# Constant products behind each item's sums on TensorE in the first ten laps

## The chip, the cores and the metric

The kernel runs on one core of a Trainium2 chip. The metric is the device time of one execution in microseconds (us). A core has five engines that run side by side and wait for each other through semaphores: TensorE (PE in the rows; PEld is its loading of weights), VectorE (DVE), ScalarE (ACT), GpSimd (POOL) and SyncE (SP). TensorE's clock is granted at one of two levels, 2.4 GHz (1.00 in the profile) and 1.2 GHz (0.50).

## What is computed

A graph layer and a mixture of experts on 12500 nodes of 256 numbers and 200000 edges that are sorted by `dst`:

```python
ft = (layernorm(x) @ W).reshape(n, 4, 64)
e = leaky_relu(sum(ft * w_att_src)[src] + sum(ft * w_att_dst)[dst])
a = exp(e - emax[dst]) / segment_sum(ex, dst)[dst] * dist
x = x + segment_sum(ft[src] * a, dst)
...
x = x + sum over the top 2 of 6 experts of gate * expert(layernorm(x))
```

Everything is float32. The part that the change touches is the segment sum.

## The kernel before

A first part of the program makes a table with one row of 264 numbers for each node and plans the work. The main stage (`main_stage`) then goes over the edges, and the last part (`experts`) over the routed tokens.

In the main stage the edges come in 196 groups of 1024 edges, which are 8 tiles of 128. A block is 128 destination nodes. An item is one group together with one block that it touches; there are 294 items, 98 times three (`HI`), and the loops hold seven such threes in their body (`TURNS`), so that each engine runs 14 laps of 21 items. An item is full when it uses all 8 tiles of its group, and half when it uses 4.

For each group GpSimd issues 8 indirect DMAs (L422) that gather the rows of `src` into one of four slots (`RING`). SyncE frees a slot when the items that use it have been weighted (L977 and L978). For item k:

- ScalarE makes `by_node`, a one-hot of the nodes for each edge (L1230, L1233), three items ahead.
- TensorE's `look_up` (L1357 to L1365) takes the scores of the destination nodes with 24 small bf16 products into the PSUM bank `m_E`. In the loop it is run for item k+2, just ahead of the sums of item k.
- VectorE adds scores (L1040), takes the exponentials from ScalarE, multiplies the gathered rows by the weights into `msg` (L1064), and makes the one-hot `by_edge` (L1026).
- TensorE's `sum_up` (L1367 to L1378) sums the messages to the nodes: 8 or 4 float32 products of 128x128 by 128x260 into columns 0 to 259 of the PSUM bank `m_A`. It is written out three times, for a full item and for either half, each behind an `If`. The last product raises the semaphore `summed`.
- VectorE adds these columns to the running sums (`add_sums`, L1080 to L1085), in its item k+2.

There are three banks `m_A`. Their upper columns are used too: 320 to 351 hold the weights `wd`, 360 to 367 the local node numbers `in_block`, both written and read by VectorE alone (L928, L929).

Between `look_up` and `sum_up` TensorE loads two words of the plan into registers and, when a pair of blocks is complete, runs one step of its router: `turn` (L1380), `router` (L1389) or `score` (L1396). So in the loop the order on TensorE is: look up item k+2, words of the plan and perhaps a router step, sum item k, look up item k+3, and so on. Each of the others is its own queue in the same order of items.

Of the kernel before, what the change touches and what calls it, by code (L numbers as in the profile page):

```python
# [8 lines left out]
ALU = mybir.AluOpType  # L9
# [12 lines left out]
NB = -(-N // P)  # L22
# [4 lines left out]
MSG = D + HEADS  # L27
# [10 lines left out]
HI = CI // 2  # L38
# [5 lines left out]
READY = NODE_AT + 2 * NW  # L44
NIT = NSLOT // HI
TURNS = 7
DUE = READY + NIT + 2
REL = DUE + NIT + 1
PLAN = REL + NG
# [15 lines left out]
RSQRT_BITS = float(0x5f3759df)  # L65
assert NIT % TURNS == 0 and NG % RING == 0 and NQ * HB == NB and NQ % 2 == 0 and NCH * CI >= NI and EW == 2 * GE and NB % 2 == 0

# [823 lines left out]
def main_stage(nc, K, table, x, sched, ydram, w, out):  # L891


    with ExitStack() as ctx:
# [16 lines left out]
        r1, r2, rb = K.r1, K.r2, K.rb  # L911
# [7 lines left out]
        plan = sb("plan", [1, PLAN], I32)  # L919
# [4 lines left out]
        psA = [bank(f"A{i}") for i in range(3)]  # L924
# [72 lines left out]
        def _(dve):  # L997
# [170 lines left out]
            dve.reg_mov(done, 0)  # L1168
            with nc.Fori(0, NIT // TURNS, engines=(mybir.EngineType.DVE,), hint_back_edge=True) as lap:
                for turn_of_lap in range(TURNS):  # L1170
                    it = lap * TURNS + turn_of_lap
                    for i in range(HI):
# [29 lines left out]
        def _(act):  # L1202
# [90 lines left out]
            act.reg_mov(routed, 0)  # L1293
            with nc.Fori(0, NIT // TURNS, engines=(mybir.EngineType.Activation,), hint_back_edge=True) as lap:
                for turn_of_lap in range(TURNS):
                    it = lap * TURNS + turn_of_lap
# [22 lines left out]
                    now = count(done)  # L1319
                    act.load([due_pairs], plan[0:1, bass.ds(it + DUE, 1)])  # L1320
                    act.reg_alu(due_now, due_pairs, 0, ALU.max)
# [25 lines left out]
        @block.tensor  # L1347
        def _(pe):
            t = nc.tensor
            words = [[pe.alloc_register(f"pe_word{q}{i}") for i in range(2)] for q in range(3)]  # L1350
            done, routed, ready_pairs, due_pairs, due_now = [
                pe.alloc_register("pe_" + n) for n in ("done", "routed", "ready", "due", "due_now")]

            def fetch(q, k):
                pe.load(words[q], plan[0:1, bass.ds(k * 2 + LOOK_AT, 2)])

            def look_up(k, i, b):  # L1357

                pe.wait_ge(node_onehots, k + 1)
                for j in range(GT):  # L1360
                    for n in range(3):
                        m = t.matmul(psE[i][:, 8 * j:8 * j + 8], by_node[i][:, j * P:(j + 1) * P],  # L1362
                                     look_parts[:, bass.ds(b, 1), 8 * n:8 * n + 8].rearrange("p a n -> p (a n)"),
                                     start=(n == 0), stop=(n == 2))
                m.then_inc(looked_up, 1)  # L1365

            def sum_up(k, i, half):  # L1367


                for case, tiles in ((0, range(GT)), (1, range(GT // 2, GT)), (2, range(GT // 2))):  # L1370
                    with pe.If(half == case):
                        pe.wait_ge(edge_onehots, k + 1)
                        pe.wait_ge(weighted, k + 1)
                        pe.wait_ge(added, k + 1)
                        for j in tiles:
                            m = t.matmul(psA[i][:, 0:MSG], by_edge[i][:, j, :], msg[i][:, j, :],  # L1376
                                         start=(j == tiles[0]), stop=(j == tiles[-1]))
                        m.then_inc(summed, 1)  # L1378

            def turn(pair):  # L1380

                pe.wait_ge(y_made, pair + 1)
                for c in range(2):
                    for i in range(2):
                        m = t.transpose(psT[:, c * 2 * P + i * P:c * 2 * P + (i + 1) * P], y[:, i, c * P:(c + 1) * P],
                                        K.ident[:, :])
                m.then_inc(y_turned, 1)

            def router(pair):  # L1389
                pe.wait_ge(y_copied, pair + 1)  # L1390
                pe.wait_ge(lg_copied, pair + 1)
                for c in range(2):
                    m = t.matmul(psR[:, 0:2 * P], r1[:, c, :], yT[:, c, :], start=(c == 0), stop=(c == 1))
                m.then_inc(rh_made, 1)

            def score(pair):  # L1396
                pe.wait_ge(rh_copied, pair + 1)
                pe.wait_ge(lg_copied, pair + 1)
                for i in range(2):
                    m = t.matmul(ps_logits[:, i, 0:NX], rhT[:, i * P:(i + 1) * P], r2[:, :], start=True, stop=True)  # L1400
                m.then_inc(logits, 1)

            def route(pair):
                turn(pair)
                router(pair)
                score(pair)

            count = lambda r: pe.snap(r, min_val=0, max_val=NPAIR)
            index = lambda r: pe.snap(r, min_val=0, max_val=NPAIR - 1)

            pe.wait_ge(ready, 1)

            t.nop().then_inc(summed, 1)
            for i in (1, 2):
                t.matmul(psA[i][:, 0:MSG], sums[:, 0, 0:P], sums[:, 0, :], start=True, stop=True).then_inc(summed, 1)
            t.nop().then_inc(y_turned, 1)
            t.nop().then_inc(lg_copied, 1)
            pe.wait_ge(plan_in, 16)
            pe.wait_ge(look_steps, 7)
            pe.wait_ge(weights_in, 16 * ROUTER_LOADS)  # L1420
            first = [pe.alloc_register(f"pe_first{i}") for i in range(2)]
            for i in range(2):
                pe.load([first[i]], plan[0:1, NODE_AT + 2 * i + 1:NODE_AT + 2 * i + 2])
                look_up(i, i, pe.snap(first[i], min_val=0, max_val=NB))
            fetch(0, 0)
            pe.reg_mov(done, 0)
            pe.reg_mov(routed, 0)
            with nc.Fori(0, NIT // TURNS, engines=(mybir.EngineType.PE,), hint_back_edge=True) as lap:
                for turn_of_lap in range(TURNS):
                    it = lap * TURNS + turn_of_lap  # L1430
                    for i in range(HI):
                        k = it * HI + i
                        half = pe.snap(words[i][0], min_val=0, max_val=2)
                        look_up(k + 2, (i + 2) % 3, pe.snap(words[i][1], min_val=0, max_val=NB))
                        fetch((i + 1) % 3, k + 1)
                        if i == 0:
                            pe.load([ready_pairs], plan[0:1, bass.ds(it + READY, 1)])
                            ready_now = count(ready_pairs)
                            with pe.If(count(routed) < count(done)):
                                turn(index(routed))  # L1440
                        if i == 1:
                            with pe.If(count(routed) < count(done)):
                                router(index(routed))
                        if i == 2:
                            with pe.If(count(routed) < count(done)):
                                score(index(routed))
                                pe.reg_mov(routed, index(routed) + 1)
                            with pe.If(count(done) < ready_now):
                                pe.reg_mov(done, index(done) + 1)
                        sum_up(k, i, half)  # L1450
                    now = count(done)
                    pe.load([due_pairs], plan[0:1, bass.ds(it + DUE, 1)])
                    pe.reg_alu(due_now, due_pairs, 0, ALU.max)
                    due = count(due_now)
                    with pe.If(now < due):
                        with pe.Fori(now, due) as pair:
                            with pe.If(count(routed) < pair):
                                route(index(routed))
                            pe.reg_mov(routed, pair)
                        pe.reg_mov(done, due)  # L1460
            now = count(done)
            with pe.If(now < NPAIR):
                with pe.Fori(now, NPAIR) as pair:
                    with pe.If(count(routed) < pair):
                        route(index(routed))
                    pe.reg_mov(routed, pair)
                pe.reg_mov(done, NPAIR)
            with pe.If(count(routed) < NPAIR):
                route(index(routed))
# [488 lines left out]
```

## Time and profile before

| | us |
|---|---|
| median of 3 runs | 3129.61 |
| lowest and highest | 3122.08, 3132.09 |
| the profiled execution | 3125.72 |
| its span, first to last instruction | 3124.0 |
| main stage, first to last item's sums | 243.7 to about 2288 |

The mean granted clock over the whole span is 0.869. The main stage's records show which engine works when. A float32 product stands in the trace as two matmul records and two weight loads. Matmuls overlap, so the records' durations are longer than the distance from one start to the next, and the arguments below go by distances between starts.

### The profile page before, as it was taken

What the parts mean: (1) busy time and instruction counts of PE and PEld (TensorE: products, weight loads), DVE (VectorE), ACT (ScalarE), POOL (GpSimd) and SP (SyncE); (2) the same over time, 40 slices, a digit from 0 to 9 for tenths busy, and PEclk for the clock granted to TensorE, in tenths of its full rate; (3) what the DMA queues carried; (4) which work ended last, traced back from release to release, by engine and by line L of the source; (5) the groups of instructions that cost most, each with busy time, mean ns of one, the idle gap of its engine ahead of it and who ended that gap; (6) DMA issues with size and microseconds to landing.
All of it is one profiled execution on the core that took longest, in us unless ns stands there. A gap on an engine that the chain in (4) does not pass through costs nothing. (4 is left out here: it accounts for less than half of the span.)

```text
span 3124.0 us, 62545 instructions
## 1 busy us (share of the span) xinstructions
PE 2332.9 (75%) x15568; PEld 1888.6 (60%) x15569; DVE 1824.0 (58%) x4215; ACT 1467.0 (47%) x2676; POOL 2095.2 (67%) x2064
## 2 busy tenths in 40 slices
PE   4946667767777777777777777777739999899995
PEld 3725555555556555666565666656637877777774
DVE  6855444555566666677777777777769333332232
ACT  2513223334444454455555666556625554444442
POOL 0046777777777777777777776666406777777775
PEclk9966777877878888889989998988869999999997
DMA  5645555555655666666666656555550445455443
GB/s 173 193 120 152 161 159 163 173 171 168 175 173 173 177 180 176 184 188 183 191 183 178 186 179 182 169 171 163 136 95 9 82 79 81 77 81 83 79 77 46
DMA packets 231876, 450.52 MB, mean 144 GB/s; under 512 B 55818, under 2 KB 148782, under 8 KB 230769
## 3 DMA queue, kind: packets, MB, share of 16 engines
q0 software_dynamic: 114816, 265.53, 36.5%
q1 hardware_dynamic: 76616, 140.14, 14.1%
q10 hardware_dynamic: 39924, 38.86, 3.8%
q8 instruction: 213, 3.49, 0.5%
q14 instruction: 307, 2.51, 0.3%
HBM read 376.74 MB, written 69.01 MB: 143 GB/s over the span
## 5 line engine op out<-in xcount | busy, mean ns | idle before, releaser
L422 POOL DMA_INDIRECT rows<-table,src_col x1568 | 1505.2, 960 | 559.8 <-issue 460.9
L1376 PE MATMUL m_A<-m_msg,m_by_edge 128*128 128x260 f32 x3920 | 1169.1, 461 | 262.6 <-issue 194.0
L1376 PEld LDWEIGHTS m_A<-m_msg,m_by_edge 128*128 128x128 f32 x3920 | 888.6, 233 | 455.7 <-issue 263.7
L1230 ACT ACTIVATE m_apart<-drow,nid 128x1024 bf16 x297 | 341.0, 1148 | 654.1 <-SPq L963 577.2
L1064 DVE TENSOR_TENSOR m_msg<-rows,m_A 128x2048 f32<-128x2048 f32 (+1 forms) x294 | 568.0, 1932 | 111.4 <-issue 103.4
L1584 POOL DMA_INDIRECT out<-x_con,x_to_i x206 | 329.2, 1598 | 105.8 <-issue 79.8
L1362 PEld LDWEIGHTS m_E<-m_look_parts,m_by_node 128*128 128x128 bf16 x7104 | 231.6, 97 | 271.0 <-issue 234.2
L1362 PE MATMUL m_E<-m_look_parts,m_by_node 128*128 x7104 | 245.3, 167 | 187.6 <-ACT m_by_node L1233 180.8
L1040 DVE TENSOR_TENSOR m_z<-m_E,rows 128x64 f32<-128x64 f32 x295 | 65.7, 223 | 486.2 <-PE m_E L1362 363.1
L1233 ACT ACTIVATE m_by_node<-m_apart,m_one 128x1024 bf16<-128x1024 bf16 x297 | 341.0, 1148 | 9.7
L1026 DVE TENSOR_TENSOR m_by_edge<-m_A,row 128x1024 f32<-128x1024 f32 (+1 forms) x295 | 306.8, 1040 | 0.4 <-issue 0.2
L1751 DVE TENSOR_TENSOR x_con<-x_X,x_b 128x512 f32<-128x512 f32 x103 | 71.3, 692 | 392.6 <-DMA out<-x_con,x_to_i 359.3
L1575 POOL DMA_INDIRECT x_yr<-ydram,x_from_i x206 | 205.1, 995 | 65.9 <-issue 62.1
L1810 ACT ACTIVATE x_h<-x_H,x_b 128x256 f32<-128x256 f32 x206 | 86.6, 471 | 298.4 <-PE x_H L1865 298.4
L1238 ACT ACTIVATE m_z<-m_z 128x32 f32<-128x32 f32 x295 | 67.3, 228 | 338.9 <-issue 174.2
L1865 PE MATMUL x_H<-x_yT,x_c 128*128 128x256 f32 x824 | 202.2, 389 | 11.7 <-issue 8.4
L1876 PE MATMUL x_X<-x_c,x_h 128*128 128x256 f32 x824 | 196.5, 382 | 3.0 <-DVEq L1758 3.0
L1865 PE MATMUL x_G<-x_h,x_c 128*128 128x256 f32 x824 | 194.7, 379 | 0.0
L1800 ACT ACTIVATE x_c<-x_w 128x512 f32 x309 | 182.7, 627 | 6.0 <-DVEq L1732 5.1
L1865 PEld LDWEIGHTS x_H<-x_yT,x_c 128*128 128x128 f32 x824 | 149.7, 192 | 42.9 <-issue 26.2
L1876 PEld LDWEIGHTS x_X<-x_c,x_h 128*128 128x128 f32 x824 | 157.6, 191 | 25.0 <-issue 3.4
L1865 PEld LDWEIGHTS x_G<-x_h,x_c 128*128 128x128 f32 x824 | 156.6, 190 | 21.3
(246 smaller groups left out, 2257.3 us busy)
## 6 DMA issues: line engine op xcount, KB each, us to landing
drow<-edges SPq DMA_DIRECT2D x196, 512.0 KB
rows<-table,src_col POOLq DMA_INDIRECT x1568
table<-f_rowbuf SPq DMA_DIRECT2D x14, 924.0 KB, 4.9
ydram<-m_y ACTq DMA_DIRECT2D x49, 264.0 KB
m_xb<-in_x ACTq DMA_DIRECT2D x48, 256.0 KB
out<-m_x ACTq DMA_DIRECT2D x48, 256.0 KB
f_xin<-in_x SPq DMA_DIRECT2D x13, 896.0 KB, 7.0
x_w<-in_L_ffn_expert_w SPq DMA_DIRECT2D x18, 256.0 KB, 5.7
```

The source lines that it names most:

```text
L422: nc.gpsimd.indirect_dma_start(K.rows[:, g % RING, j, :], None, table, bass.IndirectOffsetOnAxis(ap=K.src_col[:, g, j:j + 1], axis=0)).the ...
L1026: v.tensor_tensor(by_edge[q][:, tiles, :], in_block[q][:, tiles].unsqueeze(2).broadcast_to([P, n, P]), K.row[:, :].unsqueeze(1).broadcast_ ...
L1064: v.tensor_tensor(msg[i][:, tiles, 0:D].rearrange("p j (h n) -> p j h n", h=HEADS), rws[:, tiles, 0:D].rearrange("p j (h n) -> p j h n", h ...
L1230: a.activation(apart[i][:, :], drow[:, bass.ds(g % RING, 1), :].rearrange("p a n -> p (a n)"), ACT.Abs, bias=K.nid[:, bass.ds(b, 1)], scal ...
L1233: a.activation(by_node[i][:, :], apart[i][:, :], ACT.Relu, bias=one[:, 0:1], scale=-1.0)\
L1362: m = t.matmul(psE[i][:, 8 * j:8 * j + 8], by_node[i][:, j * P:(j + 1) * P], look_parts[:, bass.ds(b, 1), 8 * n:8 * n + 8].rearrange("p a ...
L1376: m = t.matmul(psA[i][:, 0:MSG], by_edge[i][:, j, :], msg[i][:, j, :], start=(j == tiles[0]), stop=(j == tiles[-1]))
L1575: g.indirect_dma_start(yr[t % YR][:, i, :], None, ydram, bass.IndirectOffsetOnAxis(ap=from_i[:, 2 * t + i:2 * t + i + 1], axis=0))\
L1584: g.indirect_dma_start(out, bass.IndirectOffsetOnAxis(ap=to_i[:, 2 * t + i:2 * t + i + 1], axis=0), con[t % CR][:, i, :], None, bounds_che ...
L1800: a.activation(into[t % 2][:, :, :].rearrange("p c n -> p (c n)"), of[:, bass.ds(expert(t), 1), :, :].rearrange("p e c n -> p (e c n)"), A ...
L1865: i = t_.matmul(ps[t % 2][:, m * TILE:(m + 1) * TILE], weight[t % 2][:, c, m * P:(m + 1) * P], of[t % 2][:, c, :], start=(c == 0), stop=(c ...
L1876: m = t_.matmul(psX[t % 2][:, i * D:(i + 1) * D], h2[t % 2][:, c, i * P:(i + 1) * P], c3[t % 2][:, c, :], start=(c == 0), stop=(c == 1))
```

## The change

TensorE's loop over laps becomes a function that is called twice, for laps 0 to 9 with `warm` true and for laps 10 to 13 with `warm` false. With `warm`, `sum_up` issues behind the 8 products of a full item 22 more, behind the 4 of a half item 7 more. Each is 128x128 by 128x252 in float32: the stationary side is the identity matrix, the moving side the first 252 numbers of each row of the router's weights `r1`. They write columns 260 to 511 of the bank that the item's sums went to. The semaphore `summed` is raised by the last of them and no longer by the last sum. The loop's body is otherwise the same and is indented by one step.

```diff
+WARM_LAPS = 10
+FULL_BUSY, HALF_BUSY = 22, 7
...
+            flat = lambda a: a.rearrange("p c n -> p (c n)")
...
-            def sum_up(k, i, half):
+            def keep_busy(i, n):
+
+                for _ in range(n):
+                    m = t.matmul(psA[i][:, MSG:512], K.ident[:, :], flat(r1[:, :, :])[:, 0:512 - MSG], start=True, stop=True)
+                return m
+
+            def sum_up(k, i, half, warm):
...
                             m = t.matmul(psA[i][:, 0:MSG], by_edge[i][:, j, :], msg[i][:, j, :],
                                          start=(j == tiles[0]), stop=(j == tiles[-1]))
+                        if warm:
+                            m = keep_busy(i, FULL_BUSY if case == 0 else HALF_BUSY)
                         m.then_inc(summed, 1)
...
-            with nc.Fori(0, NIT // TURNS, engines=(mybir.EngineType.PE,), hint_back_edge=True) as lap:
...
+            def laps(first, last, warm):
+                with nc.Fori(first, last, engines=(mybir.EngineType.PE,), hint_back_edge=True) as lap:
...
+            laps(0, WARM_LAPS, True)
+            laps(WARM_LAPS, NIT // TURNS, False)
```

TensorE's order at the sums of the first item of the loop's body, before. The words ahead of the arrow are what is written (`m_A0` is the first of the three banks), the last words its shape and how many stand in a row; the three pieces are the cases full, second half, first half:

```order
L1371 COMPARE_AND_BRANCH
L1376 MATMUL m_A0<-m_msg0,m_by_edge0 128x260 x8
L1371 UNCONDITIONAL_BRANCH
L1371 COMPARE_AND_BRANCH
L1376 MATMUL m_A0<-m_msg0,m_by_edge0 128x260 x4
L1371 UNCONDITIONAL_BRANCH
```

The same place now, in the laps with `warm`:

```order
L1380 COMPARE_AND_BRANCH
L1385 MATMUL m_A0<-m_msg0,m_by_edge0 128x260 x8
L1373 MATMUL m_A0<-r1,ident 128x252 x22
L1380 UNCONDITIONAL_BRANCH
L1380 COMPARE_AND_BRANCH
L1385 MATMUL m_A0<-m_msg0,m_by_edge0 128x260 x4
L1373 MATMUL m_A0<-r1,ident 128x252 x7
L1380 UNCONDITIONAL_BRANCH
```

Nothing moved; 22 and 7 products stand between an item's last sum and the next item's look-up, and a half item's path now skips 30 products of the first case where it skipped 8.

## Rows read from the trace of the kernel before

**Rows 1.** The page: span, busy us and share of the span, instructions.

```profile
span 3124.0 us, 62545 instructions
PE 2332.9 (75%) x15568; PEld 1888.6 (60%) x15569; DVE 1824.0 (58%) x4215; ACT 1467.0 (47%) x2676; POOL 2095.2 (67%) x2064
```

**Rows 2.** Busy us by engine, laps 0-9, laps 10-13, dense part of experts.

```profile
core 0: us, PE busy (x) PEld busy (x) DVE busy (x) ACT busy (x) POOL busy (x), PEclk, DMA share, GB/s
243.60:1774.90 1531.30, 1104.34 (x8272) 885.38 (x8272) 956.52 (x1951) 687.58 (x1035) 1157.19 (x1209) 0.83 0.60 175
1774.90:2288.00 513.10, 386.09 (x3252) 315.81 (x3252) 393.35 (x928) 312.75 (x474) 313.98 (x328) 0.89 0.56 162
2426.00:3088.00 662.00, 608.62 (x2856) 500.88 (x2855) 203.43 (x402) 331.19 (x717) 509.34 (x393) 1.00 0.49 79
```

**Rows 3.** POOL's gathers (L422) in laps 0-9: duration, and waits ahead of them.

```profile
L422 POOL DMA_INDIRECT rows<-table,src_col x1209: 947/953/1469, 244.4 to 1774.4; - x173
its engine sat idle before it (us, times) until:
  issue: 359.7, 1180
  SPq L978: 20.2, 29
```

**Rows 4.** TensorE's groups in laps 0-9: xcount | busy, mean ns | idle before.

```profile
L1376 PE MATMUL m_A<-m_msg,m_by_edge 128*128 128x260 f32 x2896 | 876.7, 467 | 182.1 <-issue 154.7 <-DVE m_msg L1064 14.7 <-DVE m_by_edge L1026 6.7
L1362 PE MATMUL m_E<-m_look_parts,m_by_node 128*128 x5040 | 179.0, 167 | 179.6 <-ACT m_by_node L1233 178.8
L1393 PE MATMUL m_R<-m_yT,r 128*128 128x256 f32 x112 | 34.9, 439 | 19.3 <-issue 12.3 <-ACT m_yT L1262 7.0
L1385 PE MATMUL m_T<-ident,m_y 128*128 128x128 f32 x112 | 24.2, 354 | 29.0 <-issue 29.0
L1400 PE MATMUL m_R<-r,m_rhT 128*128 128x6 f32 x112 | 17.1, 259 | 17.7 <-issue 17.7
```

**Rows 5.** TensorE in order of time, lap 2: start us, us, instructions.

```profile
804.83 5.43 PE L1376 MATMUL m_A<-m_msg,m_by_edge 128*128 128x260 f32 x16 [0.93 <-issue]
813.00 0.96 PE L1362 MATMUL m_E<-m_look_parts,m_by_node 128*128 x24 [2.73 <-ACT m_by_node L1233]
815.23 5.43 PE L1376 MATMUL m_A<-m_msg,m_by_edge 128*128 128x260 f32 x16 [1.28 <-issue]
820.50 0.75 PE L1362 MATMUL m_E<-m_look_parts,m_by_node 128*128 x24
```

**Rows 6.** TensorE in order of time, lap 9.

```profile
1708.87 0.75 PE L1362 MATMUL m_E<-m_look_parts,m_by_node 128*128 x24
1710.22 1.10 PE L1393 MATMUL m_R<-m_yT,r 128*128 128x256 f32 x4 [0.61 <-issue]
1711.16 3.67 PE L1376 MATMUL m_A<-m_msg,m_by_edge 128*128 128x260 f32 x16
1714.66 0.75 PE L1362 MATMUL m_E<-m_look_parts,m_by_node 128*128 x24
1716.04 0.58 PE L1400 MATMUL m_R<-r,m_rhT 128*128 128x6 f32 x4 [0.63 <-issue]
1717.53 1.99 PE L1376 MATMUL m_A<-m_msg,m_by_edge 128*128 128x260 f32 x8 [0.90 <-issue]
1719.36 0.75 PE L1362 MATMUL m_E<-m_look_parts,m_by_node 128*128 x24
1721.51 3.75 PE L1376 MATMUL m_A<-m_msg,m_by_edge 128*128 128x260 f32 x16 [1.40 <-issue]
```

**Rows 7.** TensorE in order of time, experts.

```profile
2504.87 1.89 PE L1865 MATMUL x_G<-x_h,x_c 128*128 128x256 f32 x8
2506.60 1.89 PE L1876 MATMUL x_X<-x_c,x_h 128*128 128x256 f32 x8
2508.32 0.60 PE L1853 MATMUL x_T<-ident,x_yr 128*128 128x128 f32 x4
```

**Rows 8.** Who waited, laps 0-9: us in total, times, longest us.

```profile
DVE m_z L1040 <- PE m_E L1362: 345.6, 111, 6.0
PE m_E L1362 <- ACT m_by_node L1233: 178.8, 84, 5.0
PE m_A L1376 <- issue: 154.7, 142, 2.1
```

**Rows 9.** The page's DMA queues: packets, MB, share.

```profile
q8 instruction: 213, 3.49, 0.5%
```

More of the change, by code:

```diff
@@ L1427, in _ @@
             pe.reg_mov(routed, 0)
-            with nc.Fori(0, NIT // TURNS, engines=(mybir.EngineType.PE,), hint_back_edge=True) as lap:
[L1429 to L1460, printed above, removed]
@@ new lines, in laps @@
+            def laps(first, last, warm):
+                with nc.Fori(first, last, engines=(mybir.EngineType.PE,), hint_back_edge=True) as lap:
+                    for turn_of_lap in range(TURNS):
+                        it = lap * TURNS + turn_of_lap
+                        for i in range(HI):
+                            k = it * HI + i
+                            half = pe.snap(words[i][0], min_val=0, max_val=2)
+                            look_up(k + 2, (i + 2) % 3, pe.snap(words[i][1], min_val=0, max_val=NB))
+                            fetch((i + 1) % 3, k + 1)
+                            if i == 0:
+                                pe.load([ready_pairs], plan[0:1, bass.ds(it + READY, 1)])
+                                ready_now = count(ready_pairs)
+                                with pe.If(count(routed) < count(done)):
+                                    turn(index(routed))
+                            if i == 1:
+                                with pe.If(count(routed) < count(done)):
+                                    router(index(routed))
+                            if i == 2:
+                                with pe.If(count(routed) < count(done)):
+                                    score(index(routed))
+                                    pe.reg_mov(routed, index(routed) + 1)
+                                with pe.If(count(done) < ready_now):
+                                    pe.reg_mov(done, index(done) + 1)
+                            sum_up(k, i, half, warm)
+                        now = count(done)
+                        pe.load([due_pairs], plan[0:1, bass.ds(it + DUE, 1)])
+                        pe.reg_alu(due_now, due_pairs, 0, ALU.max)
+                        due = count(due_now)
+                        with pe.If(now < due):
+                            with pe.Fori(now, due) as pair:
+                                with pe.If(count(routed) < pair):
+                                    route(index(routed))
+                                pe.reg_mov(routed, pair)
+                            pe.reg_mov(done, due)
```

## The prediction, made before the changed kernel ran

> **What bounds the kernel now.** The page comes first: no engine is busy for the whole span, TensorE is the highest with 75% [rows 1]. Averages over stages hide the limits, so the next view is the busy time of each engine by stretch. In laps 0 to 9, the ones that the change touches, TensorE is busy for 1104 of 1531 us at a mean clock of 0.83, VectorE for 957, ScalarE for 688, GpSimd for 1157 [rows 2]. GpSimd looks no fuller than TensorE, but its 1209 gathers stand 0.953 us each with 359.7 us of "issue" between them; 1157 + 360 = 1517 of the 1531 us, and only 20 us are waits for a slot [rows 3]. So the gathers set the pace: 1531 / 1209 x 8 = 10.1 us for a group, and TensorE's idle time is the rest that they leave it. The reader should see this in lap 2 too: TensorE waits 2.73 us ahead of a look-up for ScalarE's one-hot, which itself waits for a group, and it works at the low clock around that [rows 5].
>
> **How many items the ten laps hold.** A look-up has 24 records, so 5040 records are 210 items [rows 4]. A full item has 16 records of sums (rows 5 show it), a half one 8: 16F + 8(210 - F) = 2896 gives F = 152 full and 58 half items. This is where two records for one float32 product matter: 8 products of a full item are 16 records, so 22 added products are 44 records and 7 are 14. Added in all: 152 x 44 + 58 x 14 = 7500 records.
>
> **What one added record takes.** No row shows a record of 252 columns. At the high clock 16 records of 260 columns take from 1711.16 to the look-up's start at 1714.66, 3.50 us or 0.219 each [rows 6]. 8 records of 256 columns take 2504.87 to 2506.60, 1.73 us or 0.216 each, with a weight load ahead of each one hidden behind the one before [rows 7]. By columns both give 0.2125 us for 252. The added products have no wait and no new data, so nothing should keep them further apart. Bounds: 0.210 from a little less fixed cost, 0.219 if a record of 252 took as long as one of 260. I take 0.2125, next to the nearer row. At the low clock, 16 records take 5.43 us or more where part of them is slow [rows 5].
>
> **The sum for a full item.** 44 x 0.2125 = 9.35 us are added to 3.50 us of sums. That alone is 12.85 us against 10.1 us in which GpSimd brings a group, and look-up and issue come on top. So TensorE, which had room, has none, and it becomes the bound of these laps by a wide margin. A half item gains 14 x 0.2125 = 2.98 us on 1.75 us of sums, and it comes on top of the full item of the same group.
>
> **Why TensorE's laps are then a plain sum.** TensorE runs in order. The look-up of item k+2 stands behind the added products of item k-1, and `summed` is raised behind them too, so nobody gets anything from TensorE while they run. Each engine must then finish its own item within TensorE's: VectorE has 957 / 210 = 4.6 us of work an item, ScalarE 3.3, GpSimd 7.2 with its issue time, against an average of 12.7 for TensorE (below). The longest dependency is also short enough: VectorE starts item k when the look-up of k+1 is done and has to deliver `msg` before the sums of k, between which lie the whole sums and added products of k-1 (at least 4.7 us, when k-1 is half) and another look-up; its multiplication and what stands ahead of it take less. Queued behind VectorE's wait for `summed` are the next `by_edge` and score, both wanted one whole item later. The cover is thinnest behind a half item when a pair is being finished, 28 pairs in these laps (112 records of 4 each in rows 4); I price a miss there at up to 2 us, 56 us in all, and put it in the range.
>
> The three terms of the ten laps are:
>
> - sums: 2896 records x 0.219 = 634 us. They took 877 us of records before, at mixed clocks [rows 4]; the gain of the high clock is in this number.
> - added products: 7500 x 0.2125 = 1594 us.
> - from the look-up's start to the first sum: 0.75 us of look-up [rows 6], the idle time ahead of sums and router steps, and these steps themselves. Idle ahead of L1376, L1385, L1393 and L1400 is 182.1 + 29.0 + 19.3 + 17.7 = 248 us; I leave out waits for VectorE and ScalarE (182.1 - 154.7 = 27 and 7), which go when these have slack: 214 us, 1.02 an item. The steps are 34.9 + 24.2 + 17.1 = 76 us, 0.36 an item [rows 4]. 0.75 + 1.02 + 0.36 = 2.13 us, near the 2.15 from 1719.36 to 1721.51 and the 2.29 with a router step [rows 6]. 210 x 2.13 = 447 us. It isn't hidden by the added products, since the look-up starts right behind the sums even now and the issue gap comes after it.
>
> Idle time ahead of the look-ups, 179.6 us, was all but wholly ScalarE's one-hots [rows 4, 8], which wait for gathers; those now come early, so it goes to nothing. Together 634 + 1594 + 447 = 2675 us where 1531 us stood: **1144 us more**. The clock gives no more back than is already in the 634: in the dense part of the experts it stays at 1.00 for 662 us with TensorE 92% busy [rows 2], and here it would be busy about 90%.
>
> **The last four laps and the rest.** They keep their code. The gathers enter lap 10 with full slots, but they almost do so already (1209 issued is 151 groups in window, plus those issued ahead of it), and those laps contain more than gather time: 328 x 1.25 = 410 of 513 us. A gain there is 0 to 10 us; I take nothing. Experts and the first part don't change. So 3125.7 + 1144 = 4270 us. The profiled execution is 4 us below the median of the runs; that is inside what I can resolve.
>
> **Rivals.**
>
> 1. *The skip.* A half item now jumps over 30 products, 4 instructions each with their weight loads, 120 instead of 32. That could miss the instructions fetched ahead. Longest issue wait ahead of a sum now is 2.1 us [rows 8]; 58 x 2.1 = 122 us more, 4392 us. A fresh skip out of a full item is covered by products still in TensorE's queue, as the look-ups that start without a gap show [rows 6]. Chance 8%. The Trainium skill, page "Runtime: NRT & Kernel Launch", section "Instruction fetch mechanics", says that a taken branch whose target lies outside the two pages of 256 instructions held or being fetched forces a DMA fetch. The page's block of 16 KB agrees with the 3.49 MB in 213 packets [rows 9]. By that rule 120 instructions stay inside the window and the cost is none; the sum stays at 4270, against 4392 if it were paid each time.
>
> 2. *The clock is not held.* Constants through an identity might not bring the clock up, or gaps of 1.4 us might drop it. With the 0.83 of these laps now, the 634 + 1594 us of records become 2228 / 0.83 = 2684, 456 us more: 4726 us. Against it stands the dense stretch at 1.00 [rows 2]. Chance 5%.
>
> 3. *One record for each added product.* If they ran in a single pass, 3750 records x 0.2125 = 797 us fall off: 1878 us for the laps and 3473 us in all. All float32 products of this trace but the transposes have two records; 4 records for 4 transposes (L1853) are the only ones with one [rows 7]. An identity on the stationary side of a plain product is no transpose. Chance 5%.
>
> 4. *The other side: the added products fit into the idle time.* If the two records ran together or the filling took no more than TensorE's idle time, the gathers would go on setting the pace and the steady clock would leave only the waits for a slot and the end of the chain to be won: 1531 - 1517 = 14 us, 3112 us. It decides at a full item of 10.1 us, that is 10.1 - 3.5 - 2.1 = 4.5 us of filling, which is 22 records of 0.2125 and not 44. A half item in the group makes it less still. Chance 1%.
>
> **How the numbers follow.** The forecast of 4270 us has 81%. Its own spread: records at 0.210 or 0.219 move it by -19 or +49 us; issue gaps shorter by 0.2 us an item, or thin cover behind half items, by -40 or +56. The low end is 4215 us; the high end takes in the skip and a little of the clock, 4400 us. That leaves out about 11% with rivals 2 to 4, and some of the forecast's tails. A measurement of this kernel can tell about 0.3% from no change. Slower by more than that holds in the forecast and rivals 1 to 3, 0.98; faster 0.01, the same 0.01.
>
> **What would show it.** In the changed profile: L1373 with 7500 records, their starts 0.2125 us apart; PEclk 1.00 in laps 0 to 9, which last some 2675 us; 12.9 us from the first sum to the next look-up in a full item, 4.7 in a half one; a look-up that starts right behind the added products; GpSimd with about 1150 us of waits for slots (L978); laps 10 to 13 within 10 us of 513. The prediction is wrong if L1373 has 3750 records, if the clock falls in these laps, if a gap of 2 us or more stands ahead of each half item's sums, or if TensorE often waits for VectorE there.

## The result and the profile after

The changed kernel takes 4345.6 us (median of 4 runs, 4333.3 to 4359.0), the kernel before 3125.9 us (median of 4). The ratio is 1.391, with a 95% interval of 1.388 to 1.394. The forecast was 4270 us, with a range from 4215 to 4400.

The profiled execution has a span of 4341.0 us, 1217 more than before. The page of the changed kernel (share of the span, instructions) answers [rows 1]:

```profile
span 4341.0 us, 77546 instructions
PE 3733.0 (86%) x23068; PEld 3201.3 (74%) x23069; DVE 1826.9 (42%) x4215; ACT 1471.2 (34%) x2676; POOL 2092.4 (48%) x2064
```

TensorE has 7500 matmul records more, and all other engines the same work in a longer span. The busy time of each engine in laps 0 to 9, laps 10 to 13 and a dense part of the experts, with the granted clock, answers [rows 2]:

```profile
245.90:2999.90 2754.00, 2514.33 (x15773) 2204.61 (x15773) 965.04 (x1964) 695.29 (x1041) 1162.55 (x1216) 0.98 0.34 99
2999.90:3503.00 503.10, 376.37 (x3248) 310.40 (x3248) 385.89 (x908) 308.66 (x467) 306.69 (x320) 0.90 0.56 162
3640.00:4300.00 660.00, 607.84 (x2850) 500.40 (x2849) 203.04 (x401) 330.67 (x716) 509.37 (x394) 1.00 0.49 79
```

Laps 0 to 9 take 2754 us where they took 1531; TensorE is busy 91% of them at 0.98 of the clock. The whole loss is there: the last four laps are 7 us shorter (510.3 us before from their first sum to the end of their last, 502.9 now), the rest is as it was.

TensorE's groups in laps 0 to 9 (xcount | busy, mean ns | idle before) answer [rows 4]:

```profile
L1373 PE MATMUL m_A<-r,ident 128*128 128x252 f32 x7500 | 1639.0, 378 | 0.0
L1385 PE MATMUL m_A<-m_msg,m_by_edge 128*128 128x260 f32 x2897 | 728.2, 406 | 175.9 <-issue 173.4 <-DVE m_msg L1066 2.4
L1365 PE MATMUL m_E<-m_look_parts,m_by_node 128*128 x5040 | 158.6, 167 | 1.5 <-issue 1.5
```

The waits of VectorE and GpSimd there (us in total, times, longest us) answer [rows 3, 8]:

```profile
DVE m_z L1042 <- PE m_E L1365: 1671.9, 197, 12.7
POOL rows L424 <- SPq L980: 1224.1, 127, 21.4
```

The look-ups waited 178.8 us for one-hots before; now they stand idle for 1.5 us in all, and not for one-hots. The sums wait for VectorE once, 2.4 us. Instead everybody waits for TensorE: VectorE 1672 us for the look-up's scores, which stand behind the added products, and GpSimd 1224 us for a free slot (20 us before).

The same in order of time, in lap 4 of the changed kernel (start us, us):

```profile
1443.81 3.75 PE L1385 MATMUL m_A<-m_msg,m_by_edge 128*128 128x260 f32 x16 [0.22 <-issue]
1447.39 9.51 PE L1373 MATMUL m_A<-r,ident 128*128 128x252 f32 x44
1456.74 0.75 PE L1365 MATMUL m_E<-m_look_parts,m_by_node 128*128 x24
1459.19 2.61 PE L1385 MATMUL m_A<-m_msg,m_by_edge 128*128 128x260 f32 x8 [1.70 <-issue]
1461.59 4.25 PE L1373 MATMUL m_A<-r,ident 128*128 128x252 f32 x14
1465.68 0.75 PE L1365 MATMUL m_E<-m_look_parts,m_by_node 128*128 x24
```

A full item takes 12.93 us from its first sum to the next look-up (1443.81 to 1456.74), of which 9.35 are the 44 records of its 22 added products (1447.39 to 1456.74). The half item behind it takes 6.49 us where 4.73 were reckoned (1.75 + 2.98): its sums take 2.40 us instead of 1.75 and its 14 added records 4.09 instead of 2.98. The granted clock says why, in two stretches of that time (the first number behind POOL's busy time and its count: 0.50 and 1.00):

```profile
1460.40:1463.80 3.40, 3.40 (x10) 2.70 (x9) 1.87 (x4) 0.78 (x1) 1.90 (x2) 0.50 0.47 146
1463.80:1480.00 16.20, 15.36 (x94) 13.58 (x93) 3.87 (x7) 2.75 (x4) 12.35 (x13) 1.00 0.53 151
```

So even with all these products the clock fell to 1.2 GHz for 3.4 us, behind a look-up of 0.75 us and an idle gap of 1.70 us. That happened 33 times in laps 0 to 9, each time 2.3 to 4.3 us after the start of a look-up.

### The profile page after: what moved, and what is told of

The parts are those of the page before. It is cut to its first block and busy times, and to the rows that moved or that the text cites. A ratio compares the mean times of both kernels' runs of the same rounds, so it can differ in the third digit from the quotient of the medians.

```text
span 4341.0 us, 77546 instructions
## 1 busy us (share of the span) xinstructions
PE 3733.0 (86%) x23068; PEld 3201.3 (74%) x23069; DVE 1826.9 (42%) x4215; ACT 1471.2 (34%) x2676; POOL 2092.4 (48%) x2064
## 5 line engine op out<-in xcount | busy, mean ns | idle before, releaser
L1373 PE MATMUL m_A<-r,ident 128*128 128x252 f32 x7500 | 1639.0, 378 | 0.0
L1373 PEld LDWEIGHTS m_A<-r,ident 128*128 128x128 f32 x7500 | 1438.4, 192 | 174.8
L1385 PE MATMUL m_A<-m_msg,m_by_edge 128*128 128x260 f32 x3920 | 1012.9, 414 | 256.1 <-issue 209.0
L1385 PEld LDWEIGHTS m_A<-m_msg,m_by_edge 128*128 128x128 f32 x3920 | 779.6, 204 | 399.0 <-issue 265.1
L1365 PE MATMUL m_E<-m_look_parts,m_by_node 128*128 x7104 | 224.6, 167 | 7.5 <-issue 7.0
```

Source lines behind the costliest of these rows:

```text
L1373: m = t.matmul(psA[i][:, MSG:512], K.ident[:, :], flat(r1[:, :, :])[:, 0:512 - MSG], start=True, stop=True)
```

## The experiments

The chips differ. On two of them the kernel before itself takes 4031 and 4078 us, on the others 3123 us. Each kernel is compared with the kernel before on its own chip. On the slow ones TensorE stalls again and again, which is told at the end; of those runs I use comparisons on the same chip and the distances of undisturbed records. The runs on the other chips are `full_only` and the three whose labels end in 2.

### The changed kernel again, and the signal at the last sum

The first is the changed kernel itself. The second raises `summed` ahead of the added products:

```diff
-                        if warm:
-                            m = keep_busy(i, FULL_BUSY if case == 0 else HALF_BUSY)
                         m.then_inc(summed, 1)
+                        if warm:
+                            keep_busy(i, FULL_BUSY if case == 0 else HALF_BUSY)
```

> The changed kernel once more, on the chip of the three that follow. Both theories: about 4340 us, within 0.5% of 4346.

> The changed kernel with `summed` raised by the last sum again, ahead of the added products; nothing else differs. Theory (TensorE is full, and nobody it waits for is late): no difference, 4340 us within 15. Rival (the later signal holds VectorE's additions and with them the next item back): TensorE no longer waits, and 20 to 80 us are won, about 4290.

Measured: 4626.8 us for the changed kernel and 4616.7 us with the early signal, on a chip where the kernel before takes 4031.0. The early signal is worth 10 us, 0.2%, where 20 to 80 were the rival's. So the later `summed` is not what costs: VectorE's next step waits for the look-up, and that stands behind the added products in either case. The trace of the changed kernel says the same for a chip without stalls: nobody there waited for the added products' signal, while VectorE waited 1672 us for the look-up. The expectation of 4340 us for the first failed by the chip; laps 0 to 9 are 2853 us there against 2754, and laps 10 to 13 685 against 503.

### No product at all

`FULL_BUSY, HALF_BUSY = 0, 0`, the loop still in two calls.

> The loop in two calls of 10 and 4 laps and no added product at all. Theory (the whole change is in the products): same as before, ratio 1.000 within 0.003. Rival (the second loop's code or its start costs): some us slower.

Measured: 4069.6 us against 4078.3 on the same chip with stalls, ratio 0.998 (0.997 to 0.999). The second loop costs nothing; the loss is in the products.

### Half as many products

```diff
-FULL_BUSY, HALF_BUSY = 22, 7
+FULL_BUSY, HALF_BUSY = 11, 3
```

> 11 and 3 added products instead of 22 and 7: 3692 records. Theory (TensorE's time is the sum of its parts, two records a product, 0.2125 us each): a full item takes 3.5 + 4.7 + 2.1 = 10.3 us and a half one 1.75 + 1.3 + 2.35 = 5.4, the ten laps 1878 us and about 40 for the low clock, together 3124 + 387 = 3510 us. Rival (the added products fit beside the gathers once a full item is near 10.1 us): under 3200 us.

> 11 and 3 products once more. Theory (TensorE's time as a sum of its parts, which also bounds this case, as a full item takes 10.3 us against 10.1 for a group, and the half items come on top): 1878 us for laps 0 to 9 and some 60 for the low clock, 3510 to 3540 us. Rival (gathers hide part of it): under 3400 us.

Measured: 4273.0 us and a ratio of 1.060 on the chip with stalls; 3531.2 us and a ratio of 1.129 (1.127 to 1.132) on the clean one. The second is inside the 3510 to 3540 of the theory, with some luck: its 1878 us are the sum for 3750 records, and for these 3692 it is 634 + 785 + 447 = 1866. Laps 0 to 9 there (the row has the columns of the table above):

```profile
244.70:2204.40 1959.70, 1713.99 (x11965) 1484.51 (x11965) 964.59 (x1964) 695.10 (x1041) 1166.17 (x1215) 0.97 0.47 138
```

From this to the changed kernel 3808 records are added and 2754.0 - 1959.7 = 794 us: 0.2086 us each, against the 0.2125 at which they follow each other. With 11 and 3 products TensorE is already the bound: GpSimd waits 437.7 us for slots, where it was 20.2 before, and a full item's 8.26 us from sums to look-up and 2.0 to 2.1 behind it are just over the gathers' 10.1. So each product from there on costs its full 0.42 us.

### No products behind half items

```diff
-                        if warm:
-                            m = keep_busy(i, FULL_BUSY if case == 0 else HALF_BUSY)
+                        if warm and case == 0:
+                            m = keep_busy(i, FULL_BUSY)
```

> 22 added products behind full items only, none behind half items. Theory (TensorE's time is the sum of its parts): the 58 x 14 records go, 173 us, and the low clock that half items bring is no less; on a chip where the changed kernel takes 4346 us this one takes 4175, and half items take 4.1 us from first sum to first sum. Rival (the far skip past 30 products costs half items time, or the 7 products keep the clock up): 4200 us or more. On a chip with the issue stalls of the earlier runs the count is by undisturbed items: half ones 4.1 us, full ones 15.0.

Measured: 4212.7 us (two executions), ratio 1.350 (1.345 to 1.354), 133 us less than the changed kernel where 171 were expected. From first sum to first sum the 58 half items take 266 us in all, 174 less than in the changed kernel (440): the 173 expected, and a quarter of them 4.07 us or less. But the 152 full items take 22 us more (2336 and 2314), and laps 10 to 13, whose code is the same, 526 us where it was 503. Is it the far skip that the rival blamed? No: from the look-up to a half item's first sum it is 2.49 us in the mean here, 2.54 in the changed kernel, where the skip is as long, and 2.62 before, where it was short. The clock is part of it: in laps 0 to 9 it stood at 1.2 GHz for 182 us here and for 116 us in the changed kernel, and some 258 of the sums' records were 0.434 us apart instead of 164, which is 20 us. So the half items' 7 products seem to have held the clock up a little. Of the 23 us in laps 10 to 13, whose code is the same but lies elsewhere in the program, 16 can be seen: in three laps one look-up is preceded by an idle gap and then broken by another of 2.1 to 3.7 us, with nothing to wait for, each time between its 20th and 21st record and one lap apart (16.1 us of issue gaps ahead of look-up records; the changed kernel has none there). The cause is open; that it is the same place of the code each time is all that the trace shows.

### The same count in bf16

```diff
-                    m = t.matmul(psA[i][:, MSG:512], K.ident[:, :], flat(r1[:, :, :])[:, 0:512 - MSG], start=True, stop=True)
+                    m = t.matmul(psA[i][:, MSG:512], flat(look_parts[:, :, :])[:, 0:P], flat(look_parts[:, :, :])[:, 0:512 - MSG], start=True, stop=True)
```

> The 22 and 7 added products of 252 columns in bf16 (both sides from the look-up's table) instead of float32. Theory (a float32 product costs two records and four passes of its columns, a bf16 one a single record and pass): 152 x 22 + 58 x 7 = 3750 records about 0.107 us apart, 8.0 us for a full and 4.85 for a half item; where a lap has more of that than the gathers need (laps 6 to 9) it is TensorE's, 1583 us for the ten laps, 52 more than before: 3176 us. Rival (the price goes by products, not by passes): above 3450 us.

> The bf16 products once more, for a chip without the issue stalls. Theory (one record and one pass for a product, 0.108 us as measured): 152 full items of 8.0 us and 58 half ones of 4.85 fit into the gathers' time in laps 0 to 5 and not after them; 1583 us for laps 0 to 9, 3176 us. Rival (the time of a product is its own, whatever its type): above 3450 us.

Measured: 4238.6 us, ratio 1.041 on the chip with stalls; 3239.9 us, ratio 1.037 (1.035 to 1.039) on the clean one. All instructions of the line there:

```profile
L1373 PE MATMUL m_A<-m_look_parts x3750: 269/271/419, 249.1 to 1893.8; 128*128 128x252 bf16 x198
```

There are 3750 records for as many products, 0.108 us apart: half the records and half the distance of float32, so a product costs a quarter. Its 22 products are 2.4 us, and the loss falls from 1220 us to 117. The theory's 3176 us is 64 too low. By lap (us, from first sums to first sums): 202, 184, 175, 158, 157, 160, 153, 154, 159, 153 where the kernel before has 199, 184, 172, 160, 151, 142, 139, 130, 128, 127. Laps 0 to 3 hide the products behind the gathers as expected; from lap 4 on the laps are 6 to 31 us longer. The miss in laps 0 to 9 is 71 us (1654 against 1583). I had left out the low clock: 374 records of the sums are 0.434 us apart, 80 us. But 221 of them stand in laps 0 to 3, which are no longer for it; the 153 in laps 4 to 9 cost 33 us, about half of the miss, and the rest stays open.

Laps 0 to 3 also show directly what the clock is worth where the gathers set the pace. The row of the kernel before, then that of this run (columns as above):

```profile
243.70:958.40 714.70, 499.40 (x3321) 391.86 (x3322) 378.93 (x694) 253.02 (x373) 541.45 (x567) 0.77 0.58 168
243.01:961.30 718.29, 598.50 (x4973) 504.11 (x4974) 379.57 (x697) 256.19 (x377) 543.96 (x570) 0.91 0.58 168
```

The clock rose from 0.77 to 0.91, and the laps took 718 us where they took 715.

### The products behind the look-up

18 products behind each of the 210 look-ups in place of those behind the sums, 7560 records against 7500, written into free columns of the look-up's bank; the look-up's signal moves behind them:

```diff
+                if warm:
+                    m = keep_busy(i, FILL)
                 m.then_inc(looked_up, 1)
...
-                        if warm:
-                            m = keep_busy(i, FULL_BUSY if case == 0 else HALF_BUSY)
                         m.then_inc(summed, 1)
```

> The added products stand behind the look-up (18 behind each of the 210, 7560 records where 7500 were, into free columns of the look-up's bank), so that the look-up's short products and the gap behind it no longer follow each other. Theory (the clock drops of laps 0 to 9, 31 of them, come from that low stretch and cost about 50 us): fewer than 10 drops, 13 us for the 60 records more, 4300 us. Rival (the drops go by the idle time in all, which stays): about 30 drops and 4354 us.

> The float32 products behind the look-up once more (7560 records). In the run with issue stalls the sums of all items ran at the high clock and undisturbed full and half items took 11.85 and 10.1 us. Theory (the low clock of the changed kernel comes from the short products and the gap following each other): 152 x 11.85 + 58 x 10.15 = 2390 us for laps 0 to 9 would be even under the records' own sum of 634 + 1606 + 447 = 2687, so the period of an item is set by the kind of its neighbours; I expect 2690 to 2720 us and 4290 us in all. Rival (the clock falls as often): 2750 us or more, 4350 us.

Measured: 4801.4 us on the chip with stalls, more than the changed kernel there; on the clean one 4025.7 us, ratio 1.289 (1.287 to 1.291), **320 us less than the changed kernel with 60 records more**. Neither theory had that. The second expectation had worked out 2390 us for laps 0 to 9 from the undisturbed items of the first run, close to the 2429 measured, and put it aside for a sum with the whole gap in it. Laps 0 to 9, busy time by engine:

```profile
252.10:2681.30 2429.20, 2427.58 (x15798) 2150.16 (x15796) 960.84 (x1951) 691.10 (x1035) 1150.44 (x1205) 1.00 0.37 111
```

TensorE's groups in them:

```profile
L1387 PE MATMUL m_A<-m_msg,m_by_edge 128*128 128x260 f32 x2897 | 671.8, 383 | 1.6 <-issue 1.6
L1365 PE MATMUL m_E<-m_look_parts,m_by_node 128*128 x5040 | 157.1, 166 | 0.0
L1404 PE MATMUL m_R<-m_yT,r 128*128 128x256 f32 x112 | 28.7, 379 | 0.0
```

TensorE is busy for 2427.6 of 2429.2 us. The issue gap of 173.4 us ahead of the sums and 65 us ahead of the router steps is gone, and the clock is 1.00 throughout. In order of time:

```profile
1708.38 3.67 PE L1387 MATMUL m_A<-m_msg,m_by_edge 128*128 128x260 f32 x16
1711.89 0.75 PE L1365 MATMUL m_E<-m_look_parts,m_by_node 128*128 x24
1712.50 7.90 PE L1375 MATMUL m_E<-r,ident 128*128 128x252 f32 x36
1720.23 0.60 PE L1396 MATMUL m_T<-ident,m_y 128*128 128x128 f32 x4
```

Behind the look-up TensorE's sequencer, the part that hands instructions to the array, loads words of the plan and takes its branches. One of these loads is in the profile of the kernel before, 0.55 us each:

```profile
L1355 PEldq TENSOR_LOAD <-m_plan x295: 530/546/1161, 239.0 to 2279.4; - x148
```

From the first of these instructions to the sequencer's wait ahead of the sums it is 1.8 us in the median and 2.6 to 2.8 at most, in the kernel before, in the changed one and here alike. What differs is what the array still has to do meanwhile. In the changed kernel and in this one the sequencer begins with them when 17 matmul records that it has handed over have yet to start, in each of the 208 items looked at. In the kernel before it is 17 in 184 of them and 12 to 16 in the others. Where these 17 are the last of the look-up, they keep the array busy for 0.57 us, and about 1.1 us of the gap lie bare. Where they are added products, they last 3.97 us. Here in the stretch 1712 to 1720 of this run the load starts at 1716.6, and the sequencer is ready for the sums at 1718.5, while the added products run until 1720.2:

```profile
L1358 PEldq TENSOR_LOAD <-m_plan x1: 546/546/546, 1716.6 to 1716.6; - x1
```

So the gap isn't work of the array that must be paid, but sequencer time that lies bare because short work stands ahead of it. It is the last 17 records that cover it, not all 36. An estimate from these rows is that 14 records (2.8 / 0.2125) would do; no run tried it. The sum without the gap is 637 us from first sums to look-ups, 210 x 0.61 = 128 of look-ups, 210 x 7.73 = 1623 of products and some 45 of router steps, 2433 us, where 2429 were measured. The expectation had added the whole gap (447 us with the look-up) as if it were there.

The clock doesn't fall any more, but both the order and the idle time changed, so the run doesn't say which of them held it. It does say how little of the gain is the clock's: the changed kernel lost at most 50 us to the low clock in laps 0 to 9 (below), and this one is 325 us shorter there. Some 280 of these lie between the look-up and the sums.

The other sign on the chip with stalls, where this kernel is slower than the changed one, goes with the stalls: counted in one way, there are 46 stall phases in this kernel there and 20 in the changed one.

### A few products where there is room, and in the last laps

5 products behind full items in laps 0 to 5 alone; and 2 behind full items in laps 10 to 13 alone.

> 5 added products behind the sums of full items in laps 0 to 5 alone, where a full item then takes 3.5 + 2.1 + 2.1 = 7.7 us of the 10.1 that the gathers leave. Theory (gathers set the pace there, and a higher clock moves nothing): same as before within 0.3%, the clock of laps 0 to 5 up from 0.80, fewer or shorter low stretches, the laps as long as before within 5 us. Rival (the clock is worth time there): 10 us or more faster.

> 2 added products behind the sums of full items in laps 10 to 13 alone, where the gathers do not set the pace for all of the time. Theory (there TensorE is on the way of each item, so 4 records, 0.85 us, of a full item are added to it, less what the clock gives back): 0 to 35 us slower. Rival (the steadier clock is worth more than the products cost): up to 20 us faster.

Measured, both on a chip with stalls: ratio 1.019 (1.016 to 1.021) and 1.002 (1.001 to 1.004). The first missed the theory's "same": laps 0 to 5 took 1524 us, and 1457 on that chip with no product. But GpSimd waited some 440 us for slots in these laps even with no product, so the gathers did not set the pace, and the run doesn't say what 5 products do where they do. The nearest answer is laps 0 to 3 of the bf16 run on a clean chip: 2.4 us of products behind each full item and a higher clock left them as they were. The second is what its theory said: 11 us more in laps 10 to 13 (716.7 against 705.6). Neither shows a gain, and no kernel of this study beats the one before by more than 0.3%.

## Why the prediction held, and where it was off

The laps were reckoned at 2675 us and took 2754. From the starts of the records:

| from, to | predicted | measured |
|---|---|---|
| first sum to first added product | 634 | 692 |
| first added product to look-up | 1594 | 1607 |
| look-up to first sum | 447 | 455 |

- **Items and records.** 152 full and 58 half items, two records a product: 7500 records, right. The bf16 run shows that the count of records is the type's and not the product's.
- **0.2125 us for a record.** Right: the median is 0.212. At the low clock some were 0.42 apart, 11 us in all, which is nearly all of the 13.
- **Sums at 0.219.** This term was mis-sized by 58 us. I took the high clock for all of them. 183 of 2686 distances lie in stretches at the low clock, 164 of them at 0.434, and cost 39 us. Another 12 us are the distance from the first to the second record of an item's sums, 0.294 us in 154 of the 210 items. That occurs 111 times in the kernel before too. I had measured the sums from a row in which it does not; two rows of the same group show it (1717.53 to 1719.36 is 1.83 us for 8 records, 0.229 each) [rows 6]. The two make 51 of the 58.
- **The clock.** 0.98, held mostly and not quite: it fell 33 times, for 116 us. "If the clock falls in these laps" stood among the prediction's own signs of being wrong, and by that sign this step failed, at a small price. The rival of a clock that is not held, priced at 456 us, came in with 50.
- **2.13 us between look-up and sums.** Right at 455 / 210 = 2.17, as a fact. It was wrong to take it as fixed: the order of the work decides it, as the run with the products behind the look-up shows.
- **Nobody else is late.** Right: one wait of 2.4 us for VectorE ahead of the sums. The 56 us kept for a thin cover behind half items were not needed, and the early signal changed 0.2%. GpSimd waited 1224 us for slots where about 1150 were forecast.
- **The last laps.** 7 us shorter where 0 to 10 were allowed.
- **The skip** did not happen, as the Trainium skill's rule of the two pages in "Runtime: NRT & Kernel Launch", "Instruction fetch mechanics", has it: 120 instructions stay inside them, and the time from look-up to a half item's sums went from 2.62 to 2.54 us. No run here jumps farther than that, so where the rule begins to cost isn't shown.
- **The other side.** The point named from which the filling fits, 22 records instead of 44, is borne out from above: with 22 records of float32 (11 products) laps 0 to 9 take 428 us more than before, because half items come on top; with 22 records of bf16, half as long, the first four laps are the same and the later ones are not.

What the change was after, more clock, it got: 0.83 to 0.98. It was of no use. In the kernel before the gathers and not the array set the pace, so by the prediction's own sum even a free rise of the clock could win only the 14 us of rival 4; and laps 0 to 3 of the bf16 run, where the clock rose from 0.77 to 0.91 at almost no price, won nothing.

## What to carry to other kernels

Before filling an engine's idle time, work out the filling in the records that the trace shows (a float32 product here is two records, each as long as two of bf16, so four times a bf16 product) and hold it against the idle time of the busiest item in order, not against the mean. Speeding up an engine that waits for another wins nothing: the clock rose in laps 0 to 3 of the bf16 run, and their time stayed. And look at what stands ahead of an "issue" gap: the sequencer was 17 matmul records ahead of the array here, so long records just ahead of its loads and branches hid some 240 us that were bare behind 17 short ones.

## What the runs showed of the hardware

- Two chips of this study run the same kernel before in 4031 and 4078 us, the others in 3123. The setup and the experts take the same there (839 us from the last sums to the end in the kernel before on the fast chip, 842 in the split one on the slow one); only the main stage is longer. In the traces from there TensorE has phases of some 10 us in which one instruction starts every 0.7, 1.4, 2.1 or 2.8 us, with nothing that the profile shows it waiting for. Here in the run with no product:

```profile
1444.08 0.38 PE L1385 MATMUL m_A<-m_msg,m_by_edge 128*128 128x260 f32 x1 [1.73 <-issue]
1446.89 0.17 PE L1365 MATMUL m_E<-m_look_parts,m_by_node 128*128 x1 [2.43 <-issue]
1449.02 0.17 PE L1365 MATMUL m_E<-m_look_parts,m_by_node 128*128 x1 [1.96 <-issue]
1451.18 0.17 PE L1365 MATMUL m_E<-m_look_parts,m_by_node 128*128 x1 [1.99 <-issue]
```

  There are 80 to 100 of these in that run and 20 to 35 in the changed kernel on such a chip, by how one counts, and some nine in ten begin at the high clock. The cause is open. It makes the change look far smaller there (15% instead of 39%), and there are fewer of them with the added products; so a ratio is worth only as much as the chip on which it was taken.
- Now and then the clock fell behind a look-up of 24 small products and the gap behind it, between two long dense stretches: 33 times in 210 items of the changed kernel, 116 us at the low clock of the 2754 in laps 0 to 9. With the gap filled (the products behind the look-up) it never fell in these laps.
- TensorE's sequencer ran 17 matmul records, with their weight loads, ahead of the array: in 208 of 208 items of the changed kernel, with records 0.025 us apart, and in 208 of 208 with records 0.2125 us apart.
